# A decoder layer on one core: transposes between the two scores of a pair, and 32 places of the order tables moved

## The chip, the cores and the metric

The kernel runs on one core of a Trainium2 chip. The time is that of the device for one execution, in microseconds. A core has five engines that each work through their own instruction stream in order: TensorE (PE in the profile; its weight loads are PEld), VectorE (DVE), ScalarE (ACT), GpSimd (POOL) and SyncE (SP), which only issues DMAs here. They wait for each other by semaphores.

## What is computed

A decoder layer over 8 sequences ("blocks") of 512 positions with 256 features, in float32:

```python
x = x + attn(layernorm(x))     # layernorm again, then mamba2: in_proj, conv of 4 taps, silu,
                               # scan h = h*exp(dt*A) + dt*x*B, y = h.C + D*x, gate, out_proj
x = x + xattn(layernorm(x), ctx, ctx, adj, mask)   # 16 heads of 16:
#   scores = Q K^T / 4 + adj; scores[mask == 0] = -inf; softmax; out = weights V; out Wo + bo
x = x + ffn(layernorm(x))      # 8 experts, chosen by position: y = x W[e(s)]^T + b[e(s)]
```

The scan is done in chunks of 128 positions, 4 a block.

## The kernel before

**What a block is made of.** Attention of a block is 64 units: 4 query tiles of 128 rows times 16 heads. A unit is one 128 x 512 score tile. TensorE makes it (`score`, the matmul of line 501 on `q_st` and `k_st` into one of three banks `ps`), VectorE adds adjacency and mask and takes the row maximum (`take_max`, L1277, into one of four tiles `T`), ScalarE takes the exponential (L906), TensorE transposes it (`turn`, four transposes of L697 into one of two banks `pt`), ScalarE (L897) or, for 5 units in 16, VectorE (L1283) copies it to `PT` (`evac`), and for four units together TensorE multiplies with the values (`pv`, L716). `turn` comes three slots behind `score`, `pv` seven. `score(u)` needs the maximum of unit u-3 (its bank), `turn(u)` the exponential of u and the copy of u-2, `take_max(u)` the transposes of u-4, `pv` the copies of its four units.

**What sets the order.** All engines loop over the same list of slots, 64 a block. In each slot an engine does its fixed attention work first, then the stages that the tables put there. The scores of units u and u+1 are both issued in the even slot u, before that slot's `turn` (the loop is L726 to L734). All the rest (the Mamba stages of the next block, projections, query tiles, loads) are named stages: the table `STAGES` gives for each the place on each engine in ticks (20 ticks a slot, slot 0 being the block's first score; negative places lie in the block before), and `FIRST` gives other places for block 0. An engine does its stages in order of these numbers and waits where something is not ready, with all that is queued behind. So a place is not a time: what counts is which instruction comes before which.

**The stages that the change and the prediction speak of.**
- `qsplit c`: VectorE splits query tile c into a high part (a cast, L1244) and a low part (L1246); SyncE writes both to memory (`q_d`, L472), and `qin c` reads them back into the layout of the scores (`q_st`, L430, 8 DMAs). `kin g` reads the keys back (`k_st`, L423).
- `ln2r`: VectorE normalizes the input for the residual, four operations from SBUF to SBUF (L1072); GpSimd adds the input (L1379); SyncE then loads the next block's input (L411).
- `dt2 3`: six small operations of VectorE that end with `dA` (L1121). `dmask c` on GpSimd (L1393, two operations of 128 x 1024) waits for it.
- `conv` and `silu`: a column tile's taps on VectorE (L1259, L1262) or GpSimd (L1361, L1365, L1368), then tanh on ScalarE and a product on VectorE (L1267).
- `gate c` (L1201) makes `yg`, which `o c` transposes on TensorE (L620). `xq c` (L1226) normalizes a query tile, and `q1 c` transposes it (L634). `state c` is L1188 on VectorE. `am c` turns a mask tile into numbers (L1142). `dt1` reads its bank `pm` at L1076.

After the last block's attention comes the expert stage, which the change does not touch.

Of the kernel before, what the change touches and what calls it, by code (L numbers as in the profile page):

```python
# [25 lines left out]
B, S, E = 8, 512, 256  # L26
# [10 lines left out]
UNITS = C * AH  # L37
# [4 lines left out]
LAG = 3  # L42
# [23 lines left out]
def conv_split(b):  # L66
# [22 lines left out]
    ("seg", 0, 0): {"pe": -590, "act": -595}, ("seg", 1, 0): {"pe": -470, "act": -470}, ("gx", 0): {"pe": -455, "act": -460, "dve": -445, "pool": -775},  # L89
    ("z", 0): {"pe": -435, "act": -425, "dve": -385}, ("w", 0): {"dve": -440}, ("inter", 0): {"pe": -460, "dve": -645}, ("sdec", 0): {"pool": -720},  # L90
    ("intra", 0): {"pe": -390, "dve": -375}, ("state", 0): {"pe": -390, "dve": -365}, ("gate", 0): {"act": -365, "dve": -370},
    ("gate2", 0): {"dve": -350, "pool": -515}, ("o", 0): {"pe": -355, "act": -345}, ("x1", 0): {"pe": -315, "dve": -300, "pool": -385},
    ("xq", 0): {"dve": -245, "pool": -85}, ("q1", 0): {"pe": -225, "act": -260}, ("q2", 0): {"pe": -185, "act": -180},
    ("qsplit", 0): {"dve": -110, "sp": -215}, ("qin", 0): {"sp": -160}, ("dmask", 1): {"pool": -705}, ("seg", 0, 1): {"pe": -360, "act": -365},
    ("seg", 1, 1): {"pe": -370, "act": -380}, ("gx", 1): {"pe": -330, "act": -330, "dve": -330, "pool": -475},
    ("z", 1): {"pe": -275, "act": -275, "dve": -255}, ("w", 1): {"dve": -260}, ("inter", 1): {"pe": -205, "dve": -205}, ("sdec", 1): {"pool": -350},
    ("intra", 1): {"pe": -200, "dve": -185}, ("state", 1): {"pe": -130, "dve": -125}, ("gate", 1): {"act": -125, "dve": -175},
    ("gate2", 1): {"dve": -95, "pool": -275}, ("o", 1): {"pe": -145, "act": -170}, ("x1", 1): {"pe": -75, "dve": -55, "pool": -255},
    ("xq", 1): {"dve": -15, "pool": 35}, ("q1", 1): {"pe": 0, "act": -10}, ("q2", 1): {"pe": 55, "act": 45}, ("qsplit", 1): {"dve": 115, "sp": 120},
    ("qin", 1): {"sp": 200}, ("dmask", 2): {"pool": -540}, ("seg", 0, 2): {"pe": -105, "act": -75}, ("seg", 1, 2): {"pe": -165, "act": -180},  # L100
# [4 lines left out]
    ("q2", 2): {"pe": 455, "act": 460}, ("qsplit", 2): {"dve": 525, "sp": 465}, ("qin", 2): {"sp": 495}, ("dmask", 3): {"pool": -225},
    ("seg", 0, 3): {"pe": 115, "act": 90}, ("seg", 1, 3): {"pe": 250, "act": 255}, ("gx", 3): {"pe": 160, "act": 150, "dve": 170, "pool": 275},
    ("z", 3): {"pe": 120, "act": 130, "dve": 140}, ("w", 3): {"dve": 300}, ("inter", 3): {"pe": 310, "dve": 310}, ("sdec", 3): {"pool": 50},
    ("intra", 3): {"pe": 315, "dve": 315}, ("state", 3): {"pe": 690, "dve": 585}, ("gate", 3): {"act": 320, "dve": 330},
    ("gate2", 3): {"dve": 370, "pool": 380}, ("o", 3): {"pe": 340, "act": 320}, ("x1", 3): {"pe": 370, "dve": 395, "pool": 450},
    ("xq", 3): {"dve": 460, "pool": 1120}, ("q1", 3): {"pe": 535, "act": 535}, ("q2", 3): {"pe": 695, "act": 705},  # L110
    ("qsplit", 3): {"dve": 835, "sp": 610}, ("qin", 3): {"sp": 835}, ("cwb",): {"dve": -2040}, ("prep",): {"dve": -805}, ("rload",): {"sp": -445},
    ("r0",): {"act": -335}, ("r1",): {"pe": -290, "dve": -260}, ("r2",): {"pe": -200, "dve": -175}, ("r3",): {"pe": -115, "dve": -90},
# [6 lines left out]
    ("conv", 2): {"pool": -1254}, ("bc", 3): {"pe": -1220, "act": -1268}, ("conv", 3): {"pool": -1174}, ("dt2", 0): {"dve": -1700},
    ("dt2", 1): {"dve": -1665}, ("dt2", 2): {"dve": -1595}, ("dt2", 3): {"dve": -1590}, ("cum",): {"pe": -1265, "act": -1435},  # L120
    ("k", 0): {"pe": -1527, "act": -1732}, ("k", 1): {"pe": -1380, "act": -1395}, ("ksplit",): {"sp": -1025, "dve": -1374},
    ("v", 0): {"pe": -1393, "dve": -1422}, ("v", 1): {"sp": -1600, "pe": -1001, "dve": -996}, ("mask",): {"sp": -1140}, ("am", 0): {"dve": -1075},
# [74 lines left out]
def build(nc, t):  # L197
    ctx = ExitStack()
    with ctx:
# [205 lines left out]
        with nc.allow_non_contiguous_dma("vectors of weights, once"), nc.Block() as block:  # L405
# [93 lines left out]
            def _(pe):  # L499
# [1045 lines left out]
```

## Time and profile before

| | before |
|---|---|
| three runs | 1262.48, 1263.23 and 1270.4 us, median 1263.23 |
| the profiled execution | 1264.66 us; 1262.9 from first to last instruction |
| mean granted clock of TensorE | 0.975 |
| first score of the blocks at | 112.4, 236.2, 372.1, 508.2, 642.6, 777.1, 917.5, 1051.8 us |
| end of attention, start of the expert stage | about 1160 us |

A row of the timeline gives the start in us, the length in us, the engine, the line, the operation, the tiles written and read, the shapes and the number of instructions drawn together; in brackets stand the idle time of the engine before it and what ended it. Times of a block are told from block 3, whose scores run from 508.2 to 642.6 us; the other blocks from 1 to 6 repeat them.

### The profile page before, as it was taken

The numbers are of one execution on the slowest core, as the hardware profiler recorded it, in microseconds if no ns is written. First come the engines' busy times: TensorE is split into PE (matmuls) and PEld (weight loads), VectorE is DVE, ScalarE is ACT, GpSimd is POOL, SyncE is SP. The second block draws the span as 40 slices with busy tenths as digits, with TensorE's granted clock in tenths as the row PEclk, the third lists the DMA queues.
The fourth block names the chain that finished last, engine by engine and source line by source line (L and its number), as shares of the span: only waits on it lengthen the run. The fifth ranks groups of instructions, "written<-read, shape, count | busy, mean of one in ns | idle before, by whom it ended". The sixth has DMA issues, their size and how long they took to land. (4 is left out here: it accounts for less than half of the span.)

```text
span 1262.9 us, 29914 instructions
## 1 busy us (share of the span) xinstructions
PE 1128.2 (89%) x10292; PEld 831.9 (66%) x10292; DVE 1002.1 (79%) x2535; ACT 781.7 (62%) x1452; POOL 634.1 (50%) x554
## 2 busy tenths in 40 slices
PE   5487999999999999999999999999999999877387
PEld 2255677777777677767777777767776777765144
DVE  5866888788879887888888887888888887754486
ACT  2224676667766677667766766767566776766242
POOL 4573466337823584456643774278245653300475
PEclk9798999999999999999999999999999999999699
DMA  7042105310432024401540052103340143120511
GB/s 207 0 117 76 51 8 141 118 31 26 118 91 87 26 69 100 123 5 39 139 129 15 26 151 81 64 26 105 75 122 4 46 96 105 26 56 10 209 79 57
DMA packets 101524, 96.52 MB, mean 76 GB/s; under 512 B 17184, under 2 KB 76832, under 8 KB 100096
## 3 DMA queue, kind: packets, MB, share of 16 engines
q1 hardware_dynamic: 92912, 76.42, 20.2%
q0 software_dynamic: 6240, 17.57, 5.9%
q8 instruction: 85, 1.39, 0.5%
q10 hardware_dynamic: 2224, 0.62, 0.2%
q14 instruction: 63, 0.52, 0.1%
HBM read 71.49 MB, written 27.26 MB: 78 GB/s over the span
## 5 line engine op out<-in xcount | busy, mean ns | idle before, releaser
L906 ACT ACTIVATE T<-T,nmx 128x512 f32<-128x512 f32 x512 | 369.6, 725 | 216.3 <-DVE nmx L1277 213.6
L1277 DVE CUSTOM_DVE_ANT_0 T<-ps,am 128x512 f32<-128x512 f32 x512 | 346.5, 685 | 106.5 <-PE ps L501 104.8
L697 PE MATMUL pt<-ident,T 128*128 128x128 f32 x2048 | 310.8, 276 | 14.9 <-ACT PT L897 13.7
L697 PEld LDWEIGHTS pt<-ident,T 128*128 128x128 f32 x2048 | 249.2, 142 | 98.5 <-issue 39.4
L501 PE MATMUL ps<-k_st,q_st 128*128 128x512 f32 x512 | 196.9, 466 | 26.3 <-DMA q_st<-q_d 25.1
L897 ACT COPY PT<-pt 128x512 f32<-128x512 f32 x352 | 201.7, 573 | 14.1 <-PE pt L697 13.9
L1393 POOL TENSOR_TENSOR dmask<-triu,dA 128x1024 fp32r<-128x1024 f32 x64 | 133.3, 2147 | 50.0 <-DVE dA L1121 49.9
L716 PE MATMUL po<-PT,va 128*17 128x128 f32 x4096 | 136.7, 274 | 13.7 <-issue 7.0
L501 PEld LDWEIGHTS ps<-k_st,q_st 128*128 128x128 f32 x512 | 84.0, 192 | 65.4 <-DMA q_st<-q_d 28.8
L716 PEld LDWEIGHTS po<-PT,va 128*17 128x17 f32 x4096 | 102.0, 97 | 36.9 <-issue 35.9
L1368 POOL TENSOR_TENSOR xc<-xc,ygT 128x512 f32<-128x512 f32 x90 | 118.6, 1318 | 13.3
L1431 POOL TENSOR_TENSOR rr<-se,nhalf 128x1 f32<-128x1 f32 x32 | 22.2, 694 | 202.9 <-DVE se L1207 183.6
L1283 DVE COPY PT<-pt 128x512 f32<-128x512 f32 x160 | 109.7, 686 | 6.8 <-PE pt L697 6.1
L501 PE MATMUL pm<-xnT,wxbc 128*128 128x512 f32 x192 | 96.0, 624 | 5.1 <-ACT zt L828 2.5
L1365 POOL TENSOR_SCALAR ygT<-pre,cw 128x512 f32<-128x512 f32 x90 | 70.9, 788 | 5.9
L1403 POOL TENSOR_TENSOR xdt<-xt,dt 128x512 f32<-128x512 f32 x32 | 38.4, 1200 | 70.3 <-ACT xt L846 56.9
L501 PEld LDWEIGHTS pm<-xdt,L 128*128 128x128 f32 x512 | 60.3, 192 | 6.8 <-issue 3.2
L501 PE MATMUL pm<-xdt,L 128*128 128x64 f32 x512 | 61.0, 272 | 1.4 <-issue 0.9
L501 PE MATMUL pm<-wz,xnT 128*128 128x512 f32 x128 | 60.4, 594 | 0.4 <-ACT pre L808 0.3
L501 PE MATMUL pm<-wout,ygT 128*128 128x256 f32 x256 | 60.7, 380 | 0.0
L501 PEld LDWEIGHTS pm<-xnT,wxbc 128*128 128x128 f32 x192 | 34.3, 199 | 32.0 <-issue 31.9
L1161 DVE TENSOR_TENSOR L<-L,Gm 128x1024 f32<-128x1024 f32 x32 | 47.9, 1496 | 7.9 <-POOL xw L1413 7.8
(218 smaller groups left out, 1952.5 us busy)
## 6 DMA issues: line engine op xcount, KB each, us to landing
k_st<-k_d SPq DMA_DIRECT2D x256, 64.0 KB, 2.2
q_st<-q_d SPq DMA_DIRECT2D x256, 64.0 KB, 2.4
am<-in_mask SPq DMA_DIRECT2D x8, 1024.0 KB, 5.4
k_d<-kp SPq DMA_DIRECT2D x32, 256.0 KB, 2.6
am<-in_adj POOLq DMA_DIRECT2D x8, 1024.0 KB, 10.7
q_d<-qp SPq DMA_DIRECT2D x128, 64.0 KB, 1.6
xio<-in_x SPq DMA_DIRECT2D x8, 512.0 KB, 4.4
xio<-in_ctxT SPq DMA_DIRECT2D x8, 512.0 KB, 4.2
```

The source lines that it names most:

```text
L501: return pe.matmul(out, lhsT, rhs, start=first, stop=last)
L697: ins = pe.transpose(pt[u % 2][:, kt * P:(kt + 1) * P], T[:, u % RING, kt * P:(kt + 1) * P], ident[:, :])
L716: ins = pe.matmul(po[VT * hh:VT * hh + VW, g * P:(g + 1) * P], vas[a % 2][:, kt, g * HG + hh, :], PT[:, n % 2, hh, kt, :], start=(kt == 0) ...
L897: act.copy(PT[:, n % 2, v % HG, :, :].rearrange("p k i -> p (k i)"), pt[v % 2][:, :]).then_inc(sems["evac_act"], 1)
L906: act.activation(T[:, u % RING, :], T[:, u % RING, :], ACT.Exp, bias=nmx[:, u % RING:u % RING + 1], scale=-1.0).then_inc(sems["probs"], 1)
L1161: dve.tensor_tensor(L[:, :, :], L[:, :, :], Gm[:, :].rearrange("p (o i) -> p o i", o=1).broadcast_to([P, NH, P]), ALU.mult).then_inc(sems[ ...
L1277: dve.tensor_tensor_reduce(T[:, u % RING, :], ps[(a * UNITS + u) % S_BANKS][:, :], ams[a % 2][:, qt, :], -1.0, 3e38, ALU.add, ALU.min, nmx ...
L1283: dve.tensor_copy(PT[:, n % 2, v % HG, :, :].rearrange("p k i -> p (k i)"), pt[v % 2][:, :]).then_inc(sems["evac_dve"], 1)
L1365: pool.tensor_scalar(tap[:, :, :].rearrange("p k i -> p (k i)"), src[:, j:j + S], cw[:, mt, j:j + 1], 0.0, ALU.mult, ALU.add).then_inc(sem ...
L1368: pool.tensor_tensor(xc[:, mt, :], xc[:, mt, :], tap[:, :, :].rearrange("p k i -> p (k i)"), ALU.add).then_inc(sems["conv_pool"], 1)
L1393: pool.tensor_tensor(dmask[:, hl, :, :], triu[:, :].rearrange("p (o i) -> p o i", o=1).broadcast_to([P, NH, P]), dA2[:, hl, c, :].bitcast( ...
L1403: pool.tensor_tensor(xdt[:, :, :], xt[:, :, :], dt[:, c, :].rearrange("p (h o) -> p h o", o=1).broadcast_to([P, NH, HD]), ALU.mult).then_i ...
```

## The change

In TensorE's loop the transposes of a slot move between the two scores of that slot's pair. In the tables 32 places move. Most of the numbers move no instruction past another. Those that do: on VectorE `qsplit 2` goes ahead of the maximum of unit 26 (from behind the copy of unit 23); `ln2r` goes behind the maximum of unit 29 (from ahead of that of 28, so that `dt2 3` comes before it); `state 1` goes behind `qsplit 0`; `gate 3` goes ahead of `xq 2`; `am 1` and `am 2` join `am 0`; `silu 2` follows `silu 1`. On TensorE `state 1` goes behind score 59, and the route stage `r3` and `seg 1 3` move a few slots. On ScalarE `silu 5` moves from slot 31 to slot 22, and `gate 1` behind the exponential of unit 58. On SyncE block 0's `qin 0` goes ahead of `kin 1`, and the context load ahead of `kin 0`. The counts of instructions stay as they are. The line numbers of the kernel after are 5 higher, behind the loop 6.

```diff
-    ("ln1",): {"dve": -1130, "pool": -1180}, ("ln2",): {"dve": -1070}, ("ln2r",): {"dve": -725, "pool": -695, "sp": -325},
+    ("ln1",): {"dve": -1130, "pool": -1180}, ("ln2",): {"dve": -1070}, ("ln2r",): {"dve": -700, "pool": -670, "sp": -300},
...
                     if 0 <= a < B and u % 2 == 0:
                         score(a, u)
+                    b, v = divmod(s_ - LEAD - LAG, UNITS)
+                    if 0 <= b < B:
+                        turn(b, v)
+                    if 0 <= a < B and u % 2 == 0:
                         score(a, u + 1)
-                    a, v = divmod(s_ - LEAD - LAG, UNITS)
-                    if 0 <= a < B:
-                        turn(a, v)
```

Three places of the order follow, as the rows of one engine's stream. On VectorE, slots 25 to 27 of block 3, before (the product of `silu 4`, the maximum of unit 26, the copy of unit 23, the two operations of `qsplit 2`, the maximum of unit 27):

```order
L1267 SCALAR_TENSOR_TENSOR xc<-th,xc 128x512
L1277 ISA T,nmx<-ps,am 128x512
L1277 ISA nmx 128x1
L1283 COPY PT<-pt 128x512
L1244 CAST qp<-qf 128x256
L1246 TENSOR_TENSOR qp<-qf,qp 128x256
L1277 ISA T,nmx<-ps,am 128x512
```

and after the change:

```order
L1273 SCALAR_TENSOR_TENSOR xc<-th,xc 128x512
L1250 CAST qp<-qf 128x256
L1252 TENSOR_TENSOR qp<-qf,qp 128x256
L1283 ISA T,nmx<-ps,am 128x512
L1283 ISA nmx 128x1
L1289 COPY PT<-pt 128x512
```

The two operations of the query tile stand directly behind the product now, ahead of the maximum and the copy.

On VectorE, slots 27 to 30 of block 3, before (the taps of `conv 1`, `ln2r`, the maximum of unit 28, `dt2 3`, the maximum of unit 29):

```order
L1262 SCALAR_TENSOR_TENSOR xc<-pre,cw,xc 128x512 x3
L1072 TENSOR_SCALAR xnr<-xio,mv,rs 128x256 x4
L1277 ISA T,nmx<-ps,am 128x512
L1277 ISA nmx 128x1
L1108 SCALAR_TENSOR_TENSOR dts<-dts 128x32
L1110 SCALAR_TENSOR_TENSOR dts<-dts 128x32
L1115 SCALAR_TENSOR_TENSOR dt<-dts 128x32
L1117 TENSOR_TENSOR dA<-dt,nega 128x32
L1119 CAST dA<-dA 128x32
L1121 TENSOR_TENSOR dA<-dA 128x32
L1277 ISA T,nmx<-ps,am 128x512
```

and after the change, from the third operation of `dt2 3` to the copy of unit 27:

```order
L1121 SCALAR_TENSOR_TENSOR dt<-dts 128x32
L1123 TENSOR_TENSOR dA<-dt,nega 128x32
L1125 CAST dA<-dA 128x32
L1127 TENSOR_TENSOR dA<-dA 128x32
L1283 ISA T,nmx<-ps,am 128x512
L1283 ISA nmx 128x1
L1078 TENSOR_SCALAR xnr<-xio,mv,rs 128x256 x4
L1283 ISA T,nmx<-ps,am 128x512
L1283 ISA nmx 128x1
L1289 COPY PT<-pt 128x512
```

The four operations of `ln2r` stand behind `dA` and one maximum now, ahead of the maximum of unit 30 and the copy of unit 27.

On VectorE at the end of block 3, before (the maximum of unit 57, `state 1`, the maximum of unit 58, the copy of unit 55, `qsplit 0` of the next block):

```order
L1277 ISA T,nmx<-ps,am 128x512
L1277 ISA nmx 128x1
L1188 TENSOR_TENSOR state<-pm,state 128x512
L1277 ISA T,nmx<-ps,am 128x512
L1277 ISA nmx 128x1
L1283 COPY PT<-pt 128x512
L1244 CAST qp<-qf 128x256
L1246 TENSOR_TENSOR qp<-qf,qp 128x256
```

and after the change:

```order
L1283 ISA T,nmx<-ps,am 128x512
L1283 ISA nmx 128x1
L1283 ISA T,nmx<-ps,am 128x512
L1283 ISA nmx 128x1
L1289 COPY PT<-pt 128x512
L1250 CAST qp<-qf 128x256
L1252 TENSOR_TENSOR qp<-qf,qp 128x256
L1194 TENSOR_TENSOR state<-pm,state 128x512
```

`state 1` has left its place ahead of the query tile.

## Rows read from the trace of the kernel before

**Rows 1.** Busy us of each engine, TensorE clock, DMA share and GB/s, steady stretch.

```profile
600.00:800.00 200.00, 191.96 (x1765) 147.49 (x1764) 167.14 (x424) 139.10 (x260) 106.86 (x91) 1.00 0.34 95
```

**Rows 2.** What TensorE waited for from 150 to 1110 us: total us, times, longest.

```profile
PE ps L501 <- DMA q_st<-q_d: 12.7, 7, 2.2
PE pt L697 <- ACT PT L897: 7.5, 12, 1.0
PE pm L620 <- DVE yg L1201: 5.3, 7, 1.1
PE pm L501 <- DVE Bt L1152: 2.1, 7, 0.6
```

**Rows 3.** Timeline, end of block 3: start, us, engine, line, operation, [idle before, releaser].

```profile
630.37 0.69 DVE L1188 TENSOR_TENSOR state<-pm,state 128x512 f32<-128x512 f32 x1 [0.39 <-PE pm L501]
632.19 0.28 DVE L1244 CAST qp<-qf 128x256 fp32r<-128x256 f32 x1
632.96 1.77 SPq L472 DMA_DIRECT2D q_d<-qp  x4
635.94 4.67 SPq L430 DMA_DIRECT2D q_st<-q_d  x8
642.58 0.73 PE L501 MATMUL ps<-k_st,q_st 128*128 128x512 f32 x2 [1.77 <-DMA q_st<-q_d]
```

**Rows 4.** Timeline of slots 25 to 31 of block 3, VectorE, GpSimd and TensorE.

```profile
565.05 1.01 POOL L1365 TENSOR_SCALAR ygT<-pre,cw 128x512 f32<-128x512 f32 x1
565.69 0.69 DVE L1277 CUSTOM_DVE_ANT_0 T<-ps,am 128x512 f32<-128x512 f32 x1 [0.19 <-PE ps L501]
566.21 1.27 POOL L1368 TENSOR_TENSOR xc<-xc,ygT 128x512 f32<-128x512 f32 x1
566.91 0.72 DVE L1244 CAST qp<-qf 128x256 fp32r<-128x256 f32 x1
571.45 1.38 DVE L1072 TENSOR_SCALAR xnr<-xio,mv,rs 128x256 f32<-128x256 f32 x4
574.73 3.76 POOL L1393 TENSOR_TENSOR dmask<-triu,dA 128x1024 fp32r<-128x1024 f32 x2 [7.25 <-DVE dA L1121]
575.81 0.69 DVE L1283 COPY PT<-pt 128x512 f32<-128x512 f32 x1
577.21 1.07 PE L716 MATMUL po<-PT,va 128*17 128x128 f32 x32
578.48 0.77 POOL L1361 TENSOR_SCALAR xc<-pre,cw,cb 128x512 f32<-128x512 f32 x1
```

**Rows 5.** Timeline, VectorE beside GpSimd: two places where both want SBUF.

```profile
41.56 4.58 POOL L1393 TENSOR_TENSOR dmask<-triu,dA 128x1024 fp32r<-128x1024 f32 x2 [0.57 <-DVE dA L1121]
42.67 1.72 DVE L1267 SCALAR_TENSOR_TENSOR xc<-th,xc 128x512 f32<-128x512 f32 x1
44.31 2.45 DVE L1235 CAST kp<-zt 128x512 fp32r<-128x512 f32 x2
597.15 2.13 DVE L1238 TENSOR_TENSOR kp<-zt,kp 128x512 fp32r<-128x512 f32 x2
597.30 1.44 POOL L1403 TENSOR_TENSOR xdt<-xt,dt 128x512 f32<-128x512 f32 x1 [3.40 <-ACT xt L846]
```

**Rows 6.** Timeline at slot 17 of block 3, VectorE and TensorE.

```profile
541.71 0.42 DVE L1142 TENSOR_SCALAR am<-am 128x512 f32<-128x512 int32 x1
544.82 0.63 PE L620 MATMUL pm<-ident,yg 128*128 128x128 f32 x4 [0.71 <-DVE yg L1201]
545.20 0.19 DVE L1076 TENSOR_TENSOR dts<-pm,dtb 128x32 f32<-128x32 f32 x1
```

**Rows 7.** Timeline, start of block 0: SyncE's issues and the first scores.

```profile
102.45 4.15 SPq L423 DMA_DIRECT2D k_st<-k_d  x8
112.41 2.53 PE L501 MATMUL ps<-k_st,q_st 128*128 128x512 f32 x4 [4.81 <-DMA q_st<-q_d]
```

**Rows 8.** Timeline of block 7, at the score that begins query tile 2.

```profile
1113.17 0.85 PE L501 MATMUL ps<-k_st,q_st 128*128 128x512 f32 x2 [3.89 <-DMA q_st<-q_d]
```

More of the change, by code:

```diff
@@ L89 @@
[L89 to L100, printed above, removed]
@@ L105 @@
[L105 to L112, printed above, removed]
+    ("ln1",): {"dve": -1130, "pool": -1180}, ("ln2",): {"dve": -1070}, ("ln2r",): {"dve": -700, "pool": -670, "sp": -300},
@@ new lines @@
+    ("am", 3): {"dve": -930, "pool": -560}, ("silu", 4): {"act": -835, "dve": -775}, ("silu", 5): {"act": -824, "dve": -635},
+    ("silu", 0): {"act": -640, "dve": -570}, ("silu", 1): {"act": -610, "dve": -485}, ("silu", 2): {"act": -565, "dve": -483},
+    ("silu", 3): {"act": -482, "dve": -450}, ("kin", 0): {"sp": -230}, ("kin", 1): {"sp": -155}, ("kin", 2): {"sp": -103},
[3 rows of a table added]
+    ("dmask", 0): {"pool": -820}, ("seg", 0, 0): {"pe": -590, "act": -595}, ("seg", 1, 0): {"pe": -470, "act": -470},
+    ("gx", 0): {"pe": -455, "act": -460, "dve": -445, "pool": -745}, ("z", 0): {"pe": -435, "act": -425, "dve": -385}, ("w", 0): {"dve": -440},
@@ new lines @@
+    ("inter", 0): {"pe": -460, "dve": -645}, ("sdec", 0): {"pool": -688}, ("intra", 0): {"pe": -390, "dve": -375},
+    ("state", 0): {"pe": -390, "dve": -365}, ("gate", 0): {"act": -365, "dve": -370}, ("gate2", 0): {"dve": -350, "pool": -515},
+    ("o", 0): {"pe": -355, "act": -345}, ("x1", 0): {"pe": -315, "dve": -300, "pool": -385}, ("xq", 0): {"dve": -245, "pool": -201},
+    ("q1", 0): {"pe": -209, "act": -244}, ("q2", 0): {"pe": -185, "act": -180}, ("qsplit", 0): {"dve": -110, "sp": -215},
@@ new lines @@
+    ("qin", 0): {"sp": -170}, ("dmask", 1): {"pool": -705}, ("seg", 0, 1): {"pe": -360, "act": -365}, ("seg", 1, 1): {"pe": -370, "act": -380},
+    ("gx", 1): {"pe": -330, "act": -330, "dve": -330, "pool": -475}, ("z", 1): {"pe": -275, "act": -275, "dve": -255}, ("w", 1): {"dve": -260},
+    ("inter", 1): {"pe": -205, "dve": -205}, ("sdec", 1): {"pool": -350}, ("intra", 1): {"pe": -200, "dve": -185},
+    ("state", 1): {"pe": -115, "dve": -110}, ("gate", 1): {"act": -103, "dve": -175}, ("gate2", 1): {"dve": -95, "pool": -275},
@@ new lines @@
+    ("o", 1): {"pe": -125, "act": -170}, ("x1", 1): {"pe": -75, "dve": -55, "pool": -255}, ("xq", 1): {"dve": -15, "pool": 35},
+    ("q1", 1): {"pe": 0, "act": -10}, ("q2", 1): {"pe": 55, "act": 45}, ("qsplit", 1): {"dve": 115, "sp": 120}, ("qin", 1): {"sp": 190},
+    ("dmask", 2): {"pool": -526}, ("seg", 0, 2): {"pe": -105, "act": -75}, ("seg", 1, 2): {"pe": -165, "act": -180},
+    ("gx", 2): {"pe": 5, "act": 0, "dve": 35, "pool": -225}, ("z", 2): {"pe": -25, "act": -40, "dve": -5}, ("w", 2): {"dve": 65},
@@ new lines @@
+    ("inter", 2): {"pe": 70, "dve": 70}, ("sdec", 2): {"pool": -37}, ("intra", 2): {"pe": 80, "dve": 85},
+    ("state", 2): {"pe": 120, "dve": 135}, ("gate", 2): {"act": 185, "dve": 130}, ("gate2", 2): {"dve": 215, "pool": 120},
+    ("o", 2): {"pe": 140, "act": 145}, ("x1", 2): {"pe": 215, "dve": 230, "pool": 365}, ("xq", 2): {"dve": 332, "pool": 940},
+    ("q1", 2): {"pe": 355, "act": 345}, ("q2", 2): {"pe": 455, "act": 460}, ("qsplit", 2): {"dve": 514, "sp": 454}, ("qin", 2): {"sp": 485},
@@ new lines @@
+    ("dmask", 3): {"pool": -225}, ("seg", 0, 3): {"pe": 115, "act": 90}, ("seg", 1, 3): {"pe": 231, "act": 236},
+    ("gx", 3): {"pe": 160, "act": 150, "dve": 170, "pool": 275}, ("z", 3): {"pe": 120, "act": 130, "dve": 140}, ("w", 3): {"dve": 300},
+    ("inter", 3): {"pe": 310, "dve": 310}, ("sdec", 3): {"pool": 50}, ("intra", 3): {"pe": 315, "dve": 315},
+    ("state", 3): {"pe": 690, "dve": 585}, ("gate", 3): {"act": 320, "dve": 330}, ("gate2", 3): {"dve": 370, "pool": 380},
+    ("o", 3): {"pe": 340, "act": 320}, ("x1", 3): {"pe": 370, "dve": 395, "pool": 450}, ("xq", 3): {"dve": 460, "pool": 1120},
@@ L113 @@
+    ("q1", 3): {"pe": 535, "act": 535}, ("q2", 3): {"pe": 695, "act": 705}, ("qsplit", 3): {"dve": 835, "sp": 610}, ("qin", 3): {"sp": 825},
+    ("cwb",): {"dve": -2040}, ("prep",): {"dve": -805}, ("rload",): {"sp": -445}, ("r0",): {"act": -335}, ("r1",): {"pe": -290, "dve": -260},
+    ("r2",): {"pe": -200, "dve": -175}, ("r3",): {"pe": -8, "dve": 17},
 }
@@ L119 @@
[L119 to L122, printed above, removed]
@@ L123 @@
-    ("am", 1): {"dve": -1065}, ("am", 2): {"dve": -935}, ("am", 3): {"dve": -755, "pool": -845}, ("silu", 4): {"act": -1795, "dve": -1595},
-    ("silu", 5): {"act": -1610, "dve": -1445}, ("silu", 0): {"act": -1600, "dve": -1385}, ("silu", 1): {"act": -1340, "dve": -1170},
-    ("silu", 2): {"act": -1255, "dve": -1155}, ("silu", 3): {"act": -1165, "dve": -1085}, ("kin", 0): {"sp": -870}, ("kin", 1): {"sp": -615},
[1 row of a table removed]
+    ("lnT",): {"pe": -1765, "act": -1920}, ("dt1",): {"pe": -1635, "act": -1881, "dve": -1738}, ("dtT",): {"pe": -1630, "act": -1885},
@@ L127 @@
+    ("silu", 0): {"act": -1600, "dve": -1385}, ("silu", 1): {"act": -1340, "dve": -1170}, ("silu", 2): {"act": -1255, "dve": -1155},
+    ("silu", 3): {"act": -1165, "dve": -1085}, ("kin", 0): {"sp": -870}, ("kin", 1): {"sp": -605}, ("kin", 2): {"sp": -245},
[1 row of a table added]
     ("ot", 1): {"pe": 775, "act": 760}, ("op", 1): {"pe": 835, "dve": 850, "sp": 1070}, ("ot", 2): {"pe": 1165, "act": 1140},
@@ L135 @@
-    ("dmask", 1): {"pool": -1240}, ("seg", 0, 1): {"pe": -790, "act": -1006}, ("seg", 1, 1): {"pe": -818, "act": -1019},
-    ("gx", 1): {"pe": -950, "act": -1103, "dve": -871, "pool": -984}, ("z", 1): {"pe": -640, "act": -928, "dve": -535}, ("w", 1): {"dve": -510},
-    ("inter", 1): {"pe": -695, "dve": -648}, ("sdec", 1): {"pool": -615}, ("intra", 1): {"pe": -620, "dve": -476},
-    ("state", 1): {"pe": -545, "dve": -370}, ("gate", 1): {"act": -678, "dve": -440}, ("gate2", 1): {"dve": -230, "pool": -245},
@@ L139 @@
-    ("o", 1): {"pe": -440, "act": -726}, ("x1", 1): {"pe": -295, "dve": -155, "pool": -151}, ("xq", 1): {"dve": -115, "pool": 410},
-    ("q1", 1): {"pe": -40, "act": -213}, ("q2", 1): {"pe": 80, "act": 82}, ("qsplit", 1): {"dve": 200, "sp": -53}, ("qin", 1): {"sp": 245},
-    ("dmask", 2): {"pool": -330}, ("seg", 0, 2): {"pe": -475, "act": -746}, ("seg", 1, 2): {"pe": -473, "act": -734},
+    ("q1", 0): {"pe": -455, "act": -688}, ("q2", 0): {"pe": -150, "act": -308}, ("qsplit", 0): {"dve": -120, "sp": -868},
@@ new lines @@
+    ("qin", 0): {"sp": -615}, ("dmask", 1): {"pool": -1240}, ("seg", 0, 1): {"pe": -790, "act": -993},
+    ("seg", 1, 1): {"pe": -818, "act": -1019}, ("gx", 1): {"pe": -950, "act": -1103, "dve": -871, "pool": -984},
+    ("z", 1): {"pe": -640, "act": -928, "dve": -535}, ("w", 1): {"dve": -510}, ("inter", 1): {"pe": -695, "dve": -648},
+    ("sdec", 1): {"pool": -615}, ("intra", 1): {"pe": -620, "dve": -476}, ("state", 1): {"pe": -545, "dve": -370},
+    ("gate", 1): {"act": -678, "dve": -440}, ("gate2", 1): {"dve": -230, "pool": -245}, ("o", 1): {"pe": -440, "act": -726},
@@ L142 @@
+    ("x1", 1): {"pe": -295, "dve": -155, "pool": -151}, ("xq", 1): {"dve": -115, "pool": 410}, ("q1", 1): {"pe": -40, "act": -213},
+    ("q2", 1): {"pe": 80, "act": 82}, ("qsplit", 1): {"dve": 200, "sp": -53}, ("qin", 1): {"sp": 245}, ("dmask", 2): {"pool": -330},
+    ("seg", 0, 2): {"pe": -475, "act": -746}, ("seg", 1, 2): {"pe": -473, "act": -734},
     ("gx", 2): {"pe": -530, "act": -863, "dve": -366, "pool": -314}, ("z", 2): {"pe": -560, "act": -893, "dve": -415}, ("w", 2): {"dve": -240},
```

40 lines of the change are left out of this document (17 added, 23 removed), and 19 rows, old and new, of tables (FIRST, STAGES).

## The prediction

> **What bounds the kernel.** I read the busy table of a steady stretch first. In 200 us TensorE is busy 192, VectorE 167, ScalarE 139, GpSimd 107, and TensorE's granted clock is 1.00 of its upper level [rows 1]. So TensorE's stream is the bound, and what can be won between the first score (112 us) and the expert stage (1160 us) is what it waits. The list of TensorE's waits says for what [rows 2]: the first score of each block waits for its query tile (12.7 us in 7 waits, 1.8 each), a transpose for ScalarE's copy (7.5 us), the gate's transposes for `yg` (5.3 us in 7). A wait goes away only if no other stands right behind it, so each must be followed in the timeline. And since VectorE is the next busiest, a stall on VectorE counts as soon as it is longer than the lead that VectorE has over TensorE there.
>
> **The end of a block (gain).** At the end of block 3 VectorE waits 0.39 for `state 1`'s matmul and spends 0.69 on it, then come a maximum, a copy, and at 632.19 the cast of the next block's query tile. SyncE writes the tile from 632.96, reads it back from 635.94, and score 0 starts at 642.58 after TensorE has stood 1.77 us [rows 3]. The chain from cast to score has no other member, so the cast moves by what leaves its front: 0.39 + 0.69 = 1.08 us. That is less than the wait, so all of it arrives. Seven boundaries would give 7.6; at the one behind block 5 VectorE works on the routes, so I take 7.3. `r3`, put into that wait, costs nothing while the wait lasts (0.7 remain).
>
> **Slot 17 (nothing).** `gate 3` ahead of `xq 2` gives `yg` some 0.35 us earlier (one operation of the form of which `ln2r` does four in 1.38 [rows 4]), and TensorE's wait of 0.71 at 544.82 shrinks. But next on TensorE come the transposes of `q1 2`. They need a bank that `dt1` empties at 545.20 + 0.19 = 545.39, behind one more maximum, and swapping two operations ahead of it leaves that time where it is [rows 6]. The wait only moves from one instruction to the next: 0. The two mask conversions that join `am 0` are 0.42 each [rows 6], put in front of two maxima that have some lead; I take 0.1 a block, 0.7 in all, between 0 and 0.8 a block.
>
> **Block 0 and block 7 (gain).** In block 0, 4.15 us of key loads are issued ahead of the query tile's; score 0 waits 4.81 for it [rows 7]. Swapped, the tile is limited by its own way through memory, 2.98 us from write to read at the block's end [rows 3], so score 0 comes some 3 us sooner, but score 4 needs the keys that now come later. Between 0 and 3.1; I take 1.7. In block 7, where little Mamba work fills TensorE, the first score of tile 2 waits 3.89 [rows 8]. `qsplit 2` moves past a maximum and a copy, 0.69 each [rows 4] and a little less in a row: 1.3.
>
> **Transposes between the scores (small loss).** The same matmuls run in another order, and no result of the second score is wanted sooner than the transposes' own. What can be lost is where a transpose waits: then the second score waits behind it. TensorE's waits of this kind are 12 from 150 to 1110 us, 7.5 us together [rows 2], and most end in odd slots or are taken up by the next wait. I take 0.1 a block, 0.8 in all.
>
> **`qsplit 2` and `ln2r` (the large term).** Here two moves bring VectorE's operations beside GpSimd's. How the two behave together stands in [rows 5]. From 41.56 GpSimd has two `dmask` operations to do (alone 1.88 each [rows 4]). VectorE's product, issued at 42.67 during the first mask, takes 1.72 and is through at 44.39, behind that mask; the two masks with it take 4.58 instead of 3.76, so the second one waited for the product; and the first cast of the pair issued at 44.31 is held until that second mask has ended at 46.14 (the pair ends at 46.76). At 597.15 it is the same from the other side: of two subtractions in a row the GpSimd operation issued at 597.30, during the first, comes in before the second, and the two take 2.13 us around its 1.44; so in seven blocks. They hold each other up for whole operations and take turns, even within a run of VectorE's.
>
> The Trainium skill (SBUF — State Buffer, "SBUF: two separate sides") says that VectorE and GpSimd share a pair of ports as an exclusive lock, held for a whole instruction by whoever starts first. It does not say who gets it next; taken alone it leaves `ln2r` held up once, which is a rival below (about 1262). This trace shows the alternation as well, and the sum goes by that.
>
> Now the timeline of block 3 [rows 4]. Before, the cast of `qsplit 2` at 566.91 took 0.72 because GpSimd's product ran to 567.48. After, it is issued at 565.5 (maximum 26 waited 0.19 up to 565.69). GpSimd's L1365 holds until 566.06, the cast ends at 566.35, GpSimd's product goes next until 567.6, and the low half (0.4) ends at 567.95. Maximum 26 starts there, 2.2 us late; copy 23, maximum 27 and the taps follow. The query tile stood ahead of the taps before as well, with 1.1 us, so these are 1.1 late. `ln2r` (1.38) no longer stands ahead of maximum 28, so `dA` is ready 0.2 us earlier than before and GpSimd's masks start at 574.5 instead of 574.73. Maximum 29 takes 0.61; `ln2r` issues at 574.95, some 0.4 us behind the first mask. From here turns: mask to 576.4, first operation (0.35) to 576.7, mask to 578.5, second to 578.9, GpSimd's L1361 (0.77) to 579.6, third to 580, its next operation (taken as long) to 580.7, fourth to 581. Maximum 30 and copy 27 take 1.3 more: 582.3. `pv 6` needs copy 27, which was done at 576.5, and started at 577.21. So TensorE loses about 5.0 us a block here. Some comes back later in the block, where TensorE waits for GpSimd's chain of taps, which is not delayed as much: I take 0.6, between 0.3 and 1.2. That is 4.4 in six blocks and 1.1 less in block 0, whose `qsplit 2` stays: 29.7 us. Before, `ln2r` ran while GpSimd stood idle for 7.25 us [rows 4].
>
> The other moves (`silu 2`, `silu 5`, `gate 1`, context loads) stand behind GpSimd or DMA waits with lead, and I take nothing for them; the bound is a few tenths a block either way.
>
> **Sum.** 7.3 + 1.7 + 1.3 = 10.3 gained, 0.7 + 0.8 + 29.7 = 31.2 lost: 20.9 slower. The profiled execution took 1264.66, so 1285.5 on its basis; it lies 1.43 above the median of the runs, so **1284** against 1263.23, its own range 1273 to 1292.
>
> **Rivals.**
> - *Held up once.* If VectorE keeps its turn once it has it, `ln2r` ends behind the first mask with three operations in a row, at 577.8, `pv 6` waits until 579: 1.8 lost a block, less 0.6, some 8 in all, against 9 gained: 1264 less 1.4, about 1262. For it: a single operation of VectorE beside a mask is never held up longer. Against it: both places of [rows 5], where GpSimd comes in between two.
> - *No collision at `ln2r` (the other side, not slower).* If GpSimd's masks start later than `ln2r`, or operations of this shape do not disturb each other, `pv 6` comes at 577.6, 0.4 late in six blocks, and block 0 gains 0.6: 2 lost against 8.8 gained, about 1256. It decides if `ln2r` issues before the first mask does, a difference of 0.4 us. For it: all 28 operations of `ln2r` in the loop stand free of GpSimd before, so the trace shows none beside it. Against it: the mask waits for nothing but `dA` [rows 4], and a whole maximum stands between `dA` and `ln2r`.
> - *Neither move collides.* Then VectorE reaches maximum 28 sooner by `ln2r`'s 1.38, and with it goes one of the waits of the transposes for their copies (7.5 us in 12, 0.6 each [rows 2]): 8.8 + 7 x 0.6 = 13 gained, about 1250.
> - *The transposes hold back the second score* at every pair: at 0.1 us for 256 pairs 26 us more, beyond 1292.
>
> **Chances and range.** Turns taken, 0.55 (most of it over 1275.9, a fifth below); held up once 0.15; no collision at `ln2r` 0.18; neither 0.08; transposes 0.04. A measurement of this kernel can tell about 1% from no change, so the bounds are 1250.6 and 1275.9: faster 0.13, same 0.39, slower 0.48. The range 1252 to 1290 leaves out the fourth case, the lower edge of the third and the upper edge of the first.
>
> **What would show it.** In the profile after: the last of the four `ln2r` operations some 6 us behind the first mask's start, maximum 30 at a gap of 4 to 6 us, and a wait of about 5 us of TensorE for VectorE's `PT` at `pv 6` in seven blocks (wrong: all four done in under 2 us). The cast of `qsplit 2` over 0.7 with a long subtraction behind it. The first score's wait for its tile down from 1.8 to about 0.7 (wrong: unchanged). The wait for `yg` down to 0.4 with as much more at the next instruction. If `ln2r` runs free, the forecast is wrong by its largest term and the kernel is not slower.

## The result and the profile after

| | before | after |
|---|---|---|
| median of 22 runs | 1265.88 us | 1273.3 us |
| lowest and highest | 1262.48 and 1271.32 | 1267.82 and 1280.23 |
| ratio after to before | | 1.0057 (95% interval 1.0044 to 1.0071) |
| profiled execution, span | 1264.66, 1262.9 | 1274.72, 1272.9 |
| mean granted clock of TensorE, profiled execution | 0.975 | 0.971 |

The change makes the kernel 7 us slower, 0.57%. The forecast was 21 us slower: the right direction, almost three times the size. One run of e11 below, in which TensorE's granted clock was 0.556 (1886.59 us), is left out of its median and its ratio.

What TensorE waits for in the kernel after, from 150 to 1110 us (total us, times, longest), beside [rows 2]:

```profile
PE po L721 <- DVE PT L1289: 17.3, 13, 2.3
PE ps L506 <- DMA q_st<-q_d: 4.0, 4, 1.4
PE pt L702 <- ACT PT L903: 3.9, 12, 0.6
PE pm L639 <- ACT pre L814: 3.4, 6, 0.8
PE pm L625 <- DVE yg L1207: 3.0, 7, 0.8
PE pm L639 <- DVE dts L1082: 2.5, 6, 0.4
```

The wait for the query tile at a block's start has fallen from 12.7 to 4.0 us. The largest wait is new: `pv` for VectorE's copy, 17.3 us, 2.1 to 2.3 of it in each of seven blocks at `pv 6` (which multiplies units 24 to 27). New are also a wait of `q1` for ScalarE's copy `pre` (3.4 us) and one for `dts`.

The timeline of the kernel after in slots 25 to 31 of block 3, beside [rows 4] (the block starts 4.9 us later than before):

```profile
569.99 1.13 POOL L1371 TENSOR_SCALAR ygT<-pre,cw 128x512 f32<-128x512 f32 x1
570.36 0.28 DVE L1250 CAST qp<-qf 128x256 fp32r<-128x256 f32 x1
570.68 0.71 DVE L1252 TENSOR_TENSOR qp<-qf,qp 128x256 fp32r<-128x256 f32 x1
571.31 0.68 DVE L1283 CUSTOM_DVE_ANT_0 T<-ps,am 128x512 f32<-128x512 f32 x1
577.94 3.80 POOL L1399 TENSOR_TENSOR dmask<-triu,dA 128x1024 fp32r<-128x1024 f32 x2 [5.41 <-DVE dA L1127]
578.41 4.43 DVE L1078 TENSOR_SCALAR xnr<-xio,mv,rs 128x256 f32<-128x256 f32 x4
581.74 0.95 POOL L1367 TENSOR_SCALAR xc<-pre,cw,cb 128x512 f32<-128x512 f32 x1
583.36 0.68 DVE L1289 COPY PT<-pt 128x512 f32<-128x512 f32 x1
584.19 1.91 PE L721 MATMUL po<-PT,va 128*17 128x128 f32 x32 [2.28 <-DVE PT L1289]
```

`ln2r` issues 0.47 us behind the first mask and takes 4.43 us instead of 1.38, in each of the seven blocks to within 0.01. Narrower windows of the same timeline part the four operations (the last row holds the third and the fourth):

```profile
578.41 1.58 DVE L1078 TENSOR_SCALAR xnr<-xio,mv,rs 128x256 f32<-128x256 f32 x1
578.41 3.49 DVE L1078 TENSOR_SCALAR xnr<-xio,mv,rs 128x256 f32<-128x256 f32 x2
581.82 1.02 DVE L1078 TENSOR_SCALAR xnr<-xio,mv,rs 128x256 f32<-128x256 f32 x2
```

The first ends 0.15 us behind the first mask and the second 0.15 behind the second, while the masks themselves take hardly longer than before (3.80 instead of 3.76). The third is not held (0.40): GpSimd's L1367, issued 0.08 us ahead of it, lets it go first. The fourth (0.70) then ends 0.15 behind L1367, as the first two do behind the masks. The cast of `qsplit 2` is not held either (0.28; before 0.72): GpSimd's L1371, issued 0.38 us ahead of it, is still under way when the cast ends (1.13 instead of 0.69), and the low half behind it is held (0.71 instead of 0.43).

L1367 and L1371 each read one tile of data (`pre`, with a weight from `cw` for each row), where a mask reads two. That does not mean that they let VectorE pass. Just before, an operation of `dt2 2`, issued 0.11 us behind another L1371, ends 0.04 us behind it and takes 0.62 where the next of the same line and shape takes 0.19; so in blocks 1 to 6 of both kernels (each view shows that one operation alone):

```profile
567.77 0.69 POOL L1371 TENSOR_SCALAR ygT<-pre,cw 128x512 f32<-128x512 f32 x1
567.88 0.62 DVE L1111 SCALAR_TENSOR_TENSOR dts<-dts 128x32 f32<-128x32 f32 x1
568.54 0.19 DVE L1111 SCALAR_TENSOR_TENSOR dts<-dts 128x32 f32<-128x32 f32 x1
582.14 0.70 DVE L1078 TENSOR_SCALAR xnr<-xio,mv,rs 128x256 f32<-128x256 f32 x1
```

The last row is the fourth operation of `ln2r`.

Then look at the last row of the first fence: this `pv` takes 1.91 us where the one before the change took 1.07. The table by stretch of the kernel after says why (busy us and instructions by engine, then PEclk):

```profile
577.00:582.00 5.00, 4.91 (x29) 3.83 (x27) 4.89 (x9) 2.75 (x5) 4.06 (x3) 1.00 0.30 87
582.00:584.00 2.00, 0.00 (x0) 0.00 (x0) 2.00 (x6) 0.53 (x1) 1.85 (x3) 0.93 0.00 0
584.00:588.00 4.00, 3.81 (x43) 3.07 (x44) 2.35 (x8) 1.81 (x5) 3.51 (x5) 0.61 0.00 0
588.00:592.00 4.00, 4.00 (x27) 3.57 (x26) 2.82 (x8) 3.79 (x8) 3.85 (x4) 1.00 0.04 8
```

TensorE stands from 582 to 584, and in the stretch behind that its granted clock falls to the lower of its two levels, 1.2 GHz, for 3.4 us; that loses 1.7 us of TensorE's work. Read in windows of 1 us, the profile after has seven such stretches between 160 and 1120 us (at 170, 204, 310, 583, 856, 908 and 1000), the one before three (236, 372, 1113). Five of the seven stand at `pv 6` (all but 204 and 908); at `pv 6` of blocks 2 and 4 the clock stays up.

### The profile page after: what moved, and what is told of

It reads as the page before. It is cut to its first block and busy times, and to the rows that moved or that the text cites. A ratio compares the mean times of both kernels' runs of the same rounds, so it can differ in the third digit from the quotient of the medians.

```text
span 1272.9 us, 29914 instructions
## 1 busy us (share of the span) xinstructions
PE 1135.9 (89%) x10292; PEld 839.7 (66%) x10292; DVE 1018.7 (80%) x2535; ACT 782.7 (61%) x1452; POOL 633.4 (50%) x554
## 5 line engine op out<-in xcount | busy, mean ns | idle before, releaser
L702 PE MATMUL pt<-ident,T 128*128 128x128 f32 x2048 | 314.3, 277 | 15.6 <-ACT PT L903 13.4
L506 PE MATMUL ps<-k_st,q_st 128*128 128x512 f32 x512 | 255.5, 500 | 12.5 <-DMA q_st<-q_d 11.8
L721 PE MATMUL po<-PT,va 128*17 128x128 f32 x4096 | 141.2, 280 | 26.7 <-DVE PT L1289 18.2
L721 PEld LDWEIGHTS po<-PT,va 128*17 128x17 f32 x4096 | 104.6, 99 | 50.7 <-issue 49.0
L506 PEld LDWEIGHTS ps<-k_st,q_st 128*128 128x128 f32 x512 | 98.6, 193 | 38.8 <-issue 20.9
L1371 POOL TENSOR_SCALAR ygT<-pre,cw 128x512 f32<-128x512 f32 x90 | 71.4, 794 | 5.9
L506 PEld LDWEIGHTS pm<-xnT,wxbc 128*128 128x128 f32 x192 | 37.4, 200 | 38.6 <-issue 37.1
```

Source lines behind the costliest of these rows:

```text
L506: return pe.matmul(out, lhsT, rhs, start=first, stop=last)
L702: ins = pe.transpose(pt[u % 2][:, kt * P:(kt + 1) * P], T[:, u % RING, kt * P:(kt + 1) * P], ident[:, :])
L721: ins = pe.matmul(po[VT * hh:VT * hh + VW, g * P:(g + 1) * P], vas[a % 2][:, kt, g * HG + hh, :], PT[:, n % 2, hh, kt, :], start=(kt == 0) ...
L1371: pool.tensor_scalar(tap[:, :, :].rearrange("p k i -> p (k i)"), src[:, j:j + S], cw[:, mt, j:j + 1], 0.0, ALU.mult, ALU.add).then_inc(sem ...
```

## Experiments

Each time is a median, with the ratio to the kernel before on the same chip. First `ln2r` and `qsplit 2` are put back in the kernel after, each alone and both, and the transposes are moved alone in the kernel before.

```diff
# e1: the kernel after
-("ln2r",): {"dve": -700, "pool": -670, "sp": -300},
+("ln2r",): {"dve": -725, "pool": -695, "sp": -325},
# e2: the kernel after
-("qsplit", 2): {"dve": 514, "sp": 454},
+("qsplit", 2): {"dve": 525, "sp": 465},
# e3: both lines
# e4: the kernel before, with the loop of the change and its own tables
```

**e1.** 

> The kernel after with ln2r at its place of before (ahead of the maximum of unit 28, GpSimd idle); everything else of the change stays. Theory 1 (ln2r beside GpSimd's masks is the loss): the four operations take 0.41 each, TensorE's wait of 2.3 us for PT at pv 6 goes, some 1.2 to 2 us a block in seven blocks, and with it some of the stretches at the lower clock that the kernel after shows (8 from 160 to 1160 us, 4 before): 1258 to 1264 us, at or below the kernel before (1265.9). Theory 2 (the transposes between the scores, or another move, is the loss): ln2r is worth under 3 us, so 1270 to 1274.

Measured 1259.45 us, 0.9938 (0.9917 to 0.996). `ln2r` takes 1.38 us again and `pv 6` does not wait. So `ln2r` alone is worth about 14 us, more than the whole loss; the rest of the change gains 8 us. But TensorE has a wait for `L` in e1 that neither kernel had, and it waits longer for ScalarE's copies (3.9 us in the kernel after):

```profile
PE pt L702 <- ACT PT L903: 6.9, 15, 1.5
PE pm L506 <- ACT L L844: 5.8, 7, 0.8
```

**e2.** 

> The kernel after with qsplit 2 at its place of before (behind the copy of unit 23). Theory 1: the cast is not held up for long in the kernel after (1.03 us for both operations), and pv 6 is set by VectorE's chain through ln2r, whose length does not change by this; the 0.7 us of slots 26 to 28 and the 2 us at pv 6 are the same stall, so 1271 to 1275 (the kernel after 1273.3), less 1 us for what block 7 loses. The rival (my forecast's reading, qsplit 2 costs 1.1 us a block in six blocks): 1265 to 1268.

Measured 1279.74 us, 1.0103 (1.0063 to 1.0142). That is 6 us slower than the kernel after, whose interval (1.0044 to 1.0071) it just touches: the rival had the wrong sign, and my own bracket was missed too. Back at its old place the cast takes 0.99 us, since a two-input operation of GpSimd runs there, and `pv 6` waits 2.8 us instead of 2.3.

**e3.** 

> The kernel after with both ln2r and qsplit 2 at their places of before. Theory 1: like the run with ln2r alone put back, within 2 us (1258 to 1264). If both places collide and add up, it is faster than that run by 5 us or more.

Measured 1261.99 us, 0.9959 (0.9943 to 0.9976), 2.5 us behind e1. With and without `ln2r` the early `qsplit 2` comes out ahead, neither time by more than the two intervals leave open; that it costs what the forecast had is excluded.

**e4.** 

> The kernel before with only the transposes moved between the two scores. Theory 1: the second score comes 0.36 us later and no maximum with it, so the time is that of the kernel before within 2 us (1264 to 1268). Theory 2 (this order holds TensorE back): 1270 or more.

Measured 1263.09 us, 0.9977 (0.9951 to 1.0002): no loss, and no gain that is clear of the noise. In the trace the second score comes 0.36 us later and the maxima where they were.

The next four take `ln2r` alone, at a place between the two, and two other parts of the change.

```diff
# e5: the kernel before
-("ln2r",): {"dve": -725, "pool": -695, "sp": -325},
+("ln2r",): {"dve": -700, "pool": -670, "sp": -300},
# e6: the kernel after
-("ln2r",): {"dve": -700, ...
+("ln2r",): {"dve": -712, ...
# e7: e1, and
-("silu", 2): {"act": -565, "dve": -483}, ("silu", 3): {"act": -482, "dve": -450},
+("silu", 2): {"act": -565, "dve": -455}, ("silu", 3): {"act": -475, "dve": -450},
# e8: the kernel before
-("state", 1): {"pe": -130, "dve": -125}, ("gate", 1): {"act": -125, ...}, ("o", 1): {"pe": -145, ...}
+("state", 1): {"pe": -115, "dve": -110}, ("gate", 1): {"act": -103, ...}, ("o", 1): {"pe": -125, ...}
```

**e5.** 

> The kernel before with only ln2r moved, as the change moves it. Theory 1 (the collision with GpSimd's masks is the loss, whatever else moves): the four operations take over 4 us again, pv 6 waits 2 to 3 us in seven blocks, 10 to 18 us slower than the kernel before (1276 to 1284 with 1266.3). Theory 2 (ln2r loses only together with qsplit 2 or the transposes): within 4 us of the kernel before.

Measured 1294.75 us, 1.024 (1.0202 to 1.0277): 29 us slower, beyond the bracket. The four operations take the same 4.43 us, and the longest wait for VectorE's copy is 3.5 us. What is different is the clock behind it. Four stretches of e5, block 3:

```profile
585.00:587.00 2.00, 0.97 (x10) 0.73 (x8) 2.00 (x2) 0.00 (x0) 2.00 (x3) 1.00 0.30 87
587.00:590.00 3.00, 0.60 (x13) 0.58 (x17) 3.00 (x9) 0.83 (x2) 2.85 (x3) 0.66 0.00 0
590.00:595.00 5.00, 5.00 (x41) 4.16 (x31) 2.52 (x7) 3.82 (x9) 4.51 (x6) 0.52 0.01 3
595.00:600.00 5.00, 5.00 (x59) 4.33 (x57) 3.49 (x8) 3.62 (x7) 4.51 (x6) 1.00 0.02 3
```

The clock is at the lower level for nearly 7 us, 3.4 us of work lost, and so in blocks 2 to 5 each time. From 160 to 1160 us e5 loses 24 us of TensorE's work that way, the kernel before 7. So more than half of what `ln2r` costs there (17 of 29 us) is not the wait.

**e6.** 

> The kernel after with ln2r moved up on VectorE past one maximum and past dt2 3 only: behind the maximum of unit 28, ahead of the operations that give dA. VectorE does the same work in these slots; what differs is that GpSimd's masks have not begun, since they wait for dA. Theory 1: the four operations take 0.41 each, pv 6 does not wait over 0.5 us, and the time is that of the run with ln2r at its old place (1259.45) within 3 us. The rival (VectorE is simply too full between slots 26 and 31, collision or not): pv 6 still waits 1 us or more, 1265 to 1272.

Measured 1258.27 us, 0.9942 (0.992 to 0.9965). Past `dt2 3` and one maximum, with the same work in the same slots, 15 us come back:

```profile
567.79 1.38 DVE L1078 TENSOR_SCALAR xnr<-xio,mv,rs 128x256 f32<-128x256 f32 x4
570.47 3.75 POOL L1399 TENSOR_TENSOR dmask<-triu,dA 128x1024 fp32r<-128x1024 f32 x2 [6.69 <-DVE dA L1127]
573.25 1.07 PE L721 MATMUL po<-PT,va 128*17 128x128 f32 x32
```

`pv 6` starts without a wait. The collision is the cause, not the load of VectorE.

**e7.** 

> The kernel after with ln2r and the places of silu 2 and silu 3 as before. In the run with ln2r alone put back TensorE waits at slot 41 for gx 0 by 1.08 us a block (0.33 before the change), because the products silu 1 and silu 2 in a row hold GpSimd's taps up and ScalarE's silu 3 stands ahead of an exponential. Theory 1: these two places cost 0.7 us a block in seven blocks once ln2r no longer hides it, so 1252 to 1256. The rival (the wait for GpSimd's chain is there anyway): 1258 to 1261.

Measured 1252.34 us, 0.9888 (0.9857 to 0.9919), about 6 us better than e1. The wait for ScalarE's `L` is gone. Two things in the trace of e1 made it, and e7 takes both back, so that they are not parted: beside two products of VectorE in a row GpSimd's L1371 takes 1.53 us (1.01 in e7), so that the taps come later; and `silu 3`, whose tanh waits 2.49 us for them, stands ahead of an exponential and of `L`. In the kernel after there is no wait for `L`: TensorE and ScalarE are held up at `pv 6` before, and the taps are there in time.

**e8.** 

> The kernel before with only the places of state 1, gate 1 and o 1 moved, which take state 1 from ahead of qsplit 0 at the end of each block. Theory 1 (the cast moves by 1.05 us and the first score with it): seven waits of 1.8 us shrink to 0.8, 1257 to 1261 with 1266.3 for the kernel before. The rival (the tile's way through memory takes up what was won, or TensorE waits elsewhere): 1264 to 1268.

Measured 1258.62 us, 0.9944 (0.9924 to 0.9964), 7 us better than before. The wait for the query tile falls to

```profile
PE ps L501 <- DMA q_st<-q_d: 6.7, 5, 3.8
```

from 12.7 in 7 [rows 2]. The longest of the five is the first score of tile 2 in block 7, which before stands behind the end of this window [rows 8]; at the starts of blocks 2.9 us are left. That is 9.8 less, of which 7 arrive in the time, as the sum of the prediction has it.

The last four: `bc 2` and block 0's loads put back on top of e7, and TensorE filled while it waits, in e5 and in the kernel after.

```diff
# e9: e7, and
-("bc", 2): {"pe": -752, "act": -767},
+("bc", 2): {"pe": -770, "act": -785},
# e11: e7, and in FIRST
-("kin", 1): {"sp": -605}, ("qin", 0): {"sp": -615},
+("kin", 1): {"sp": -615}, ("qin", 0): {"sp": -605},
# e10: e5, in turn(a, u); e12: the kernel after, with 6 in place of 7
-for kt in range(C):
+for kt in list(range(C)) * (7 if u == 28 and a < B - 1 else 1):
```

**e9.** 

> The run with ln2r and the silus put back, and bc 2 ahead of bc 3 again on TensorE and ScalarE. In that run TensorE waits 0.8 us a block at slot 27 for ScalarE's copy of bc 2 (before the change no such wait). Theory 1: that wait is the price of bc 2's move, and putting it back gives 0.6 to 0.8 us in six blocks: 1246 to 1250 where the run with both silus back took 1252.3. The rival (bc 2 ahead of score 26 holds VectorE's chain up as much, as it did in the kernel before): 1251 to 1254.

Measured 1250.34 us, 0.9865 (0.9839 to 0.9891). The wait of `q1` for `pre` is gone; the gain over e7 is 2 us, which the two intervals do not part. This is the fastest version: 1.35% faster than the kernel before.

**e10.** 

> The kernel before with ln2r alone moved (1294.75 in its own run), and TensorE given work in the wait that follows: the four transposes of unit 28 are done seven times instead of once in seven blocks (24 more transposes of 0.109 us, 2.6 us a block, into the same bank, with the same result). VectorE's collision stays as it is, pv 6 starts when it did. In the profile of the run with ln2r alone TensorE's granted clock falls to half for 3.4 us (two stretches of 1.7 us lost) behind the wait of 3.5 us in five of seven blocks. Theory 1 (half of ln2r's price is the clock that falls after the wait): the wait of pv 6 shrinks to under 1 us, the clock stays up, 1276 to 1284, 10 us or more faster with more work. The rival (the lower clock has other causes and the wait alone is the price): 1293 to 1300.

Measured 1279.49 us, 1.0095 (1.0068 to 1.0121): 15 us faster than e5 with more work. `pv 6` of block 3 starts after a TensorE that was busy, and the clock stays up (stretches of e10, block 3):

```profile
580.00:585.00 5.00, 4.82 (x43) 4.45 (x41) 5.00 (x7) 1.25 (x3) 4.85 (x5) 1.00 0.19 53
585.00:590.00 5.00, 4.37 (x53) 3.87 (x53) 4.11 (x10) 4.47 (x10) 4.51 (x5) 1.00 0.01 2
```

Between 160 and 1160 us e10 loses 7 us to the lower clock, e5 24: 17 us between them (in e5 the lower clock stands behind the wait at `pv 6` in all seven blocks, twice as long in four; the expectation has five). The two profiled executions are 12.8 us apart, the medians 15, and by the ratios it is 18.

**e11.** 

> The run with ln2r and the silus put back, and block 0's key loads ahead of its first query tile again. My forecast took 1.7 us for that move. Theory 1 (what score 0 wins, score 4 gives back waiting for the keys): 1251 to 1254, as without it (1252.3). The rival (the 1.7 us are real): 1253.5 to 1255.

Measured 1252.38 us, 0.9891 (0.9859 to 0.9922). That is the time of e7, but the intervals leave 4 us open on either side, so the times can't tell 1.7 us from nothing. The two profiles say more. Score 0 starts at 111.13 us in e7 and at 114.17 in e11; by score 12 nearly half of that is given back (e7, then e11):

```profile
111.13 0.96 PE L506 MATMUL ps<-k_st,q_st 128*128 128x512 f32 x3 [1.89 <-DMA q_st<-q_d]
128.68 0.50 PE L506 MATMUL ps<-k_st,q_st 128*128 128x512 f32 x1
114.17 2.53 PE L506 MATMUL ps<-k_st,q_st 128*128 128x512 f32 x4 [4.90 <-DMA q_st<-q_d]
130.39 0.50 PE L506 MATMUL ps<-k_st,q_st 128*128 128x512 f32 x1
```

From there to the end of block 1 every score of e7 stands 1.7 us ahead, in blocks 2 to 5 about 1, and in the last two between 0.2 behind and 1.1 ahead. What of it reaches the end stays open.

**e12.** 

> The kernel after, whole, with the four transposes of unit 28 done six times instead of once in seven blocks (20 more transposes, 2.2 us a block, into the same bank, with the same result), so that TensorE works through the 2.3 us for which pv 6 waits. Theory 1 (part of what the change loses is the clock that falls behind this wait; it fell in 7 stretches of 1.7 us from 160 to 1120 us of the profile after, in 3 of the kernel before): 3 to 5 stretches fewer, 1264 to 1269 where the kernel after took 1273.3. The rival (a wait of 2.3 us is too short to matter for the clock): 1272 to 1276.

Measured 1261.6 us, 0.9971 (0.9955 to 0.9986): the kernel after with 140 useless transposes added is 12 us faster than without, and faster than the kernel before. More than I expected. Behind `pv 6` no stretch at the lower clock is left; from 160 to 1120 us there are two (896, 1111). By the profiles 8.5 us less of TensorE's work is lost to the clock there (five stretches of 1.7; up to 1160 us it is 6.8), and 3.6 us less is waited for the query tile at block starts. What the second has to do with the filling I can't say; that stays open.

One profile a kernel could be chance, but each run has its granted clock. The share not granted, times the span, has these means: 39.6 us in the kernel after (22 runs), 31.0 in e12 (12), 32.2 in e1 (8), 51.0 in e5 (5), 31.5 in e10 (6), 34 to 36 in the kernel before beside them. By this estimate filling the wait gave back 8.6 us in the kernel after and 19.5 in e5, and of what `ln2r` costs the kernel after 7.4 us are the clock (e1).

## Why the prediction was right in kind and wrong in size

**The large term was mis-sized.** "`qsplit 2` and `ln2r`" stood at 29.7 us; in the kernel after the two measured 11 to 12 together (e3), `ln2r` alone about 14 (e1). That `ln2r` alone costs the kernel before 29 us (e5) is the forecast's number by luck: more than half of that is the clock, which the forecast left out. Four things are in the term.
- *Turns were taken, but not every time.* The forecast had all of `ln2r`'s four operations wait for one of GpSimd's, 6 us. The first two did: they were through 2.05 and 3.96 us behind the first mask's start, where the forecast had 2.2 and 4.4. The third went ahead of L1367, and only the fourth waited for that. So GpSimd had one turn fewer, and the four took 4.43. [rows 5] shows only operations of GpSimd that read two tiles (L1393 and L1403); these came in next each time. L1367 and L1371 read one, and let one operation of VectorE go ahead before they held the next. I took the first kind for all. Why the two kinds differ is not shown.
- *`qsplit 2` was priced with the wrong sign.* For the same reason its cast was not held (0.28), the pair took 1.03 us where I had 2.4, and the move costs nothing (e2 and e3 have it 6 and 2.5 us ahead, with wide intervals) where I had 1.1 a block lost. These two errors, 1.6 and 1.4 us, make up about the difference between a wait of 5 us forecast and 2.3 measured.
- *What comes back later was taken too small.* I had 0.6 us a block, at most 1.2. By the lists of waits it is about 1.3: against e1 the kernel after waits 5.8 us less for `L` and 3.0 less for ScalarE's copies, in seven blocks.
- *The clock was not in the sum at all.* I read the granted clock of a steady stretch (1.00, [rows 1]) and took it for given. A wait that I added was priced at its length. What it measured is its length, of which later waits give back a part, and the lower clock behind it, 8.5 us by the profiles of e12 and the kernel after (17 in e5, by e10). The Trainium skill (TensorE: Matmul & The Clock Gate, "HAM oscillation — how this bites in real kernels") describes a kernel in which TensorE starts every tile at the lower clock behind a wait for data; this trace agrees in kind, with 3.4 us at the lower level behind five of the seven waits at `pv 6`. I had not looked for this where the row showed 1.00.

An estimate from these numbers: against e1 `pv` waits 15.1 us more for VectorE's copies (17.3 and 2.2), 8.8 come back, and the clock takes 7.4; that is 13.7 of the 14 us measured.

**What held.** The end of a block: 7.3 forecast, 7 measured alone (e8). The start of block 0: 1.7 forecast, and 1.7 in the profiles of e7 and e11 up to the end of block 1, though the times can't show it; that score 0 comes 3 us sooner and the next scores give some of it back was the mechanism named, the 1.7 a choice between 0 and 3.1. Slot 17: nothing, and by the mechanism named: the wait for `yg` fell from 5.3 to 3.0 us and 2.5 us came up at `q1 2` for `dts`. In the kernel after:

```profile
549.39 0.63 PE L625 MATMUL pm<-ident,yg 128*128 128x128 f32 x4 [0.38 <-DVE yg L1207]
550.43 0.41 PE L639 MATMUL pm<-ident,xnr 128*128 128x128 f32 x2 [0.41 <-DVE dts L1082]
```

The transposes between the scores: 0.8 us of loss forecast, none seen (e4). The rival without a collision at `ln2r` was priced at 1256; e1, which takes the collision away, has 1259.

**What failed beside the large term.** "The other moves ... I take nothing for them": the silus cost 6 us (e1 to e7) and `bc 2` some 2, within the noise (e7 to e9). Both are the same oversight. I followed the moved stage on VectorE or TensorE and not the queues of ScalarE and GpSimd, where `silu 3` and the copy of `bc 2` moved past other work and the taps met two products in a row. The list under "The change" lacks both: `bc 2` goes behind `bc 3` on TensorE and ScalarE, and `silu 3` ahead of an exponential on ScalarE. In block 7 `qsplit 2` was to gain 1.3 us at the score that waited 3.89 [rows 8]; in the kernel after it waits 3.70:

```profile
1125.80 0.50 PE L506 MATMUL ps<-k_st,q_st 128*128 128x512 f32 x1 [3.70 <-DMA q_st<-q_d]
```

The mask conversions (0.7 forecast) were not run alone.

**The sum as it came out**, by the ratios, of 1265.9 us: `ln2r` 15 slower; the silus nothing while `ln2r` hides them, and 6 slower without it; the end of the blocks 7 faster; `qsplit 2` 3 to 6 faster, with wide intervals; the others within 3 each. These add up to 2 to 5 slower where 7 were measured; the parts are not independent, and the noise of each is some 3 us.

## What to carry to other kernels

A move of a few instructions on VectorE is priced by what GpSimd is doing at that moment, and by which form of operation: look up in the trace a pair of just these two forms side by side before extending a pattern to a third, and look for the row that would contradict it. A wait added to a busy TensorE costs its length and, behind it, what the lower clock takes; read the clock in the stretches behind the waits that are there already, not the mean of 200 us. And when a stage is moved, follow it on each of its engines, since a hidden loss (here in ScalarE's queue) shows only when the larger one in front of it is taken away.

## What the runs showed of the hardware

- The operations of VectorE shown here, from SBUF to SBUF, waited for all of an operation of GpSimd that was under way, whether it read one tile or two: beside the masks 0.41 became 1.58 and 1.98, beside L1367 it became 0.70, each ending 0.15 us behind GpSimd's; beside L1371 0.19 became 0.62. The Trainium skill (SBUF — State Buffer, "SBUF: two separate sides") has the lock held for a whole instruction by whoever starts first; this trace agrees.
- Who starts first is not always who was issued first. A mask queued behind a VectorE operation came in before VectorE's next one; L1367 and L1371, which read one tile, let one more go ahead (0.40 and 0.28, not held).
- Between 160 and 1120 us the lower clock came in stretches of 3.4 us or twice that, each stretch of 3.4 us losing 1.7 us of TensorE's work. In the kernel after six of seven stand at waits of 2.0 to 2.3 us, but not every such wait was followed by one (`pv 6` of blocks 2 and 4). TensorE filled with transposes kept its granted clock at 1.00 through the same place (e10, e12).
- The runs of one kernel differ by this clock: the kernel after took 1267.82 us at 0.973 and 1280.23 at 0.962.
